# Attention and expert kernel: far and near scores set between the projections, far results stored ahead of the lower query and key rows

## The reference

```
x = layernorm(x + attention(x))     # 16 heads of 16 columns; query row n sees key rows n - d
                                    # for d in 0..32 and 48, 64, 96, 128, 192, 256, 384
x = layernorm(x + experts(x))       # router picks 2 of 8 experts for a row, 1024 places each
```

## Time and profile before

| | |
|---|---|
| median of three runs | 1755.79 us |
| profiled execution | 1759.34 us |
| its span, first to last instruction | 1757.6 us |
| PE busy | 1364.2 us (78%) |
| PE weight loads busy | 867.5 us (49%) |
| DVE, ACT, POOL busy | 971.1, 902.0, 712.1 us |
| mean granted clock of PE | 0.795 |

### The profile page before, as it was taken

One profiled execution on the slowest core, in us unless ns is written; L12 is line 12 of the kernel. 1 busy time (PEld: TensorE's weight loads), 2 busy tenths in 40 slices (PEclk: granted clock), 3 DMA queues, 4 the chain that ended last, 5 costly groups with the idle time before them and its releaser, 6 DMA issues. The chain is left out here.

```text
span 1757.6 us, 69086 instructions
## 1 busy us (share of the span) xinstructions
PE 1364.2 (78%) x31232; PEld 867.5 (49%) x31232; DVE 971.1 (55%) x2079; ACT 902.0 (51%) x1551; POOL 712.1 (41%) x653
## 2 busy tenths in 40 slices
PE   3567687787878878787887989788653999999960
PEld 1334454555545555454445555455331666666640
DVE  3225557565666656566565756657642555555426
ACT  5134454463646536465544745545543555555517
POOL 5123144363635436354443635444332133333346
PEclk9567686786968778687777868777766999999985
DMA  7655263443526344362534426253412344444239
GB/s 198 167 149 128 86 143 100 119 107 95 139 76 168 85 107 106 86 144 74 139 84 112 104 80 151 62 132 67 114 15 87 85 97 97 97 97 97 37 37 382
DMA packets 194695, 195.49 MB, mean 111 GB/s; under 512 B 61712, under 2 KB 178528, under 8 KB 191153
## 3 DMA queue, kind: packets, MB, share of 16 engines
q1 hardware_dynamic: 176208, 167.44, 36.0%
q0 software_dynamic: 15360, 15.10, 5.6%
q10 hardware_dynamic: 2832, 8.52, 1.2%
HBM read 115.63 MB, written 86.25 MB: 115 GB/s over the span
## 5 line engine op out<-in xcount | busy, mean ns | idle before, releaser
L415 POOL TENSOR_TENSOR p<-p 128x512 f16<-128x512 f32 x96 | 131.1, 1365 | 251.2 <-ACT p L833 251.1
L1172 POOL DMA_INDIRECT disp<-y,sidx x128 | 187.7, 1467 | 54.7 <-issue 38.1
L861 ACT COPY featT<-gp 128x1024 f16<-128x1024 f16 x96 | 93.2, 1027 | 219.1 <-PE gp L577 219.1
L1444 POOL DMA_INDIRECT xln<-y,place x64 | 103.4, 1615 | 223.9 <-DVE y L1584 205.4
L584 PE MATMUL gp<-featT,wr 128*128 128x512 f16 x768 | 188.9, 402 | 5.3 <-issue 2.9
L415 DVE TENSOR_TENSOR p<-p 128x512 f16<-128x512 f32 x96 | 82.5, 860 | 199.4 <-ACT p L833 199.4
L832 ACT ACTIVATE p<-st 128x512 f16<-128x512 f32 x192 | 117.3, 611 | 75.5 <-PE st L629 42.7
L1541 ACT ACTIVATE h<-up,v_near 128x512 f16<-128x512 f32 x128 | 88.2, 689 | 132.1 <-issue 124.0
L1594 DVE TENSOR_TENSOR h<-h 128x512 f16<-128x512 f32 x128 | 88.7, 694 | 74.1 <-ACT h L1542 74.1
L1159 POOL TENSOR_TENSOR x<-xin,x 128x1024 f16<-128x1024 f32 x16 | 34.0, 2127 | 235.3 <-ACT x L868 235.3
L584 PEld LDWEIGHTS gp<-featT,wr 128*128 128x128 f16 x768 | 74.1, 102 | 102.8 <-issue 27.8
(11 more groups left out here) (191 smaller groups left out, 3048.9 us busy)
## 6 DMA issues: line engine op xcount, KB each, us to landing
v_near<-v_dram SPq DMA_DIRECT2D x32, 528.0 KB, 8.1
qk_dram<-qk SPq DMA_DIRECT2D x64, 256.0 KB, 3.8
o_dram<-o_far SPq DMA_DIRECT2D x64, 136.0 KB, 4.5
o_back<-o_dram SPq DMA_DIRECT2D x16, 544.0 KB, 4.8
v_dram<-vs SPq DMA_DIRECT2D x16, 528.0 KB
v_far<-v_dram SPq DMA_DIRECT2D x64, 132.0 KB
disp<-y ACTq DMA_DIRECT2D x8, 1040.0 KB, 8.4
rows<-disp SPq DMA_DIRECT2D x16, 520.0 KB, 3.5
```

The lines of the kernel that those rows point to most:

```text
L415: engine.tensor_tensor(p16[:, b, 1, :], p32[:, b, :], p16[:, b, 0, :], ALU.subtract).then_inc(is_split, 1)
L861: gp_done(nc.scalar.copy(featT[:, i, :, :].rearrange("f c t -> f (c t)"), bank[:, :].bitcast(F16)), n, stage, PART_OF_T[stage], i)
L1172: nc.gpsimd.indirect_dma_start(out=disp[:, :], out_offset=bass.IndirectOffsetOnAxis(ap=sidx[:, t, k:k + 1], axis=0), in_=y16[n.par][:, t, ...
L1444: nc.gpsimd.indirect_dma_start(out=xln[:, :], out_offset=bass.IndirectOffsetOnAxis(ap=place[:, gr, t:t + 1], axis=0), in_=y[:, gr, t, :], ...
```

## The change

The tables move two parts of the scores on PE: the second far part (k = 1) from slot 0 to slot 1, and the first near part (k = 2) from slot 5 to slot 3. Their exponentials on ACT move from slots 1 and 5 to slots 2 and 4, and the far part's split on DVE and POOL from slot 2 to slot 3. The router's product `rank l` moves from the head of slot 3 to the end of slot 2 on PE; its place on ACT is kept by the `LATER` entry. On SP the far results are stored at slot 4 in place of 6, and the loads of the lower rows of `qs` and `ks` become a function of their own, called at slot 7.

```diff
-    0: [("proj", "qk0"), ("gate", "den1"), ("gate", "inv1")], 1: [("proj", "qk1"), ("gate", "mul")], 2: [("proj", "vg0")],
-    3: [("rank", "l"), ("proj", "vg1")], 4: [("outp", "t")], 5: [("rank", "c")],
+    0: [("proj", "qk0"), ("gate", "den1"), ("gate", "inv1")], 1: [("proj", "qk1"), ("gate", "mul")], 2: [("proj", "vg0"), ("rank", "l")],
+    3: [("proj", "vg1")], 4: [("outp", "t")], 5: [("rank", "c")],
...
-SCORES_AT = [-1, 0, 5, 8, 10, 12]
+SCORES_AT = [-1, 1, 3, 8, 10, 12]
...
             def head(n, h):
                 if (n.c, h) == (B, 2):
                     first_expert()
+                if h == 7 and n.shift(1).in_range():
+                    load_rest(n.shift(1))
                 if not n.in_range():
                     return
...
-                if h == 6:
+                if h == 4:
 
                     wait(sp, o_in, n.at(16))
                     sp.wait_ge(far_out, n.at(FAR_PAIRS, FAR_PAIRS))
...
                 for w in range(2):
                     sp.wait_ge(qk_split, n.at(4, 2 * w + 2))
                     store(n, w, 1, qk_lo_stored)
+            def load_rest(n):
+
                 sp.wait_ge(qk_lo_stored, n.at(32, 32))
                 for w, dst in ((0, qs), (1, ks)):
```

More of the change, by code:

```diff
@@ L67 @@
 AHEAD = {"split": 2, "feat": 2, "proj": 1, "maxp": 1, "gate0": 0, "gate": -1, "outp": -1, "rout": -1, "rank": -2}
-LATER = {("act", "proj", "vg0"): 2, ("act", "proj", "vg1"): 2, ("act", "gate", "mul"): 2, ("act", "rank", "l"): 3,
+LATER = {("act", "proj", "vg0"): 2, ("act", "proj", "vg1"): 2, ("act", "gate", "mul"): 2, ("act", "rank", "l"): 4,
          ("pool", "gate", "mul"): 2,
@@ L79 @@
          ("rank", "l"): 1, ("rank", "c"): 1}
-SCORES_AT = [-1, 0, 5, 8, 10, 12]
-EXP_AT = [[-1, 1, 5, 8, 11, 13], [0, 1, 5, 8, 11, 13]]
-SPLIT_AT = [1, 2, 6, 10, 12, 14]
+SCORES_AT = [-1, 1, 3, 8, 10, 12]
+EXP_AT = [[-1, 2, 4, 8, 11, 13], [0, 2, 4, 8, 11, 13]]
+SPLIT_AT = [1, 3, 6, 10, 12, 14]
 VALUES_AT = [2, 4, 7, 9, 13, 16]
```

## The result

The changed kernel takes 1797.45 us (median of 4 runs, 1786.54 to 1803.6), the kernel before 1754.8 us beside it on the same chip (4 runs). The ratio is 1.0226, with a 95% interval of 1.019 to 1.0263: slower by some 40 us. I had forecast 1769 us, +13. The direction was right, the size a third of what came.

The account below looks back on a forecast made before the run. PE was taken to bound the kernel, with its own work plus pauses for instruction blocks and waits. -45 + 22 + 27 + 14 - 15 + 10 = +13 us gave 1769 us; own range 1761 to 1784, whole range 1740 to 1801.

Parts of the forecast that it names:

- (1): Second far scores between the query and key projection halves: 29 us of pauses and 16 us of clock saved, -45 us.
- step 2: Ahead of qk0, PE waits out ACT's copies to featT, which far scores had covered: 1.5 us an iteration, +22 us.
- fourth rival: Slower: far scores keep their pauses wherever they stand, clock saved as taken; 1798 us, chance 0.08.
- third rival: Much slower: lower stacks hold up an instruction block in every iteration, one 2.78 us pause doubling; 1801 us, chance 0.12.
- (3): Ahead of the output projection, PE waits 2.3 us for featT's refill, which near scores had covered: +27 us.
- (4): Lower clock in vg1 behind narrow work and in the output projection behind the idle wait: +14 us.
- first rival: Faster: instruction blocks come in during the featT waits, so pauses behind the output projection shrink; 1731 us, chance 0.24.
- Step (5): On SP, far results stored and loaded back earlier, so PE waits less for DVE's maxima: -15 us.
- Step (6): Lower stacks' loads now run during near values and near scores, lengthening PE's pauses for instruction blocks: +10 us.

Follow-up runs that it names:

- e13: Kernel before, its second far scores done in 32 wider products instead of 128, the right scores of this part left out: 1710.47 us, ratio 0.9741.
- e16: e5 with the second far scores done in a quarter of the products, the right scores of this part left out: 1706.41 us, ratio 0.9706 to the kernel before.
- e5: Kernel before with only the second far scores moved, plus eight throwaway products ahead of the wait for featT before the first projection half: 1757.85 us, ratio 1.0011.
- e2: Kernel before with only the first near scores and rank l moved ahead of the second value and gate half: 1794.36 us, ratio 1.0225.
- e3: Kernel before with only SP's order changed, far results stored and loaded back ahead of the lower stacks: 1758.87 us, ratio 1.0002.
- e10: Kernel before with seven eighths of the lower stacks' loads left out from the third batch on: 1741.57 us, ratio 0.9945.
- e8: e2 with ACT's last value and gate copies put behind featT's refill and the output projection starting on the first copy: 1796.69 us, ratio 1.023.

## Why the prediction was right in direction and wrong in size

- **The step that failed is (1), "second far scores between the halves of the projection ... together -45 us"**, both of its terms. "I take 29 us as saved": the far scores' pauses fell by 13 us in the changed kernel (28.2 to 15.2), and pauses as a whole by under 5. I had read them rightly as blocks of instructions not yet there (the packets above), and then priced them as if they belonged to the far scores. They follow the count of instructions: moved work takes its blocks along (626.60 above), and fewer instructions made them 25 to 34 us shorter (e13 to e16). "Clock ... I take 16 us": 2.9 us came (97.7 to 94.8), and over the whole execution none (111.2 to 111.8), since the wait of step 2 lowers the clock just as the pause did; e5 shows the one, e13 the other. I named that wait as a reason to take 16 and not 22, which was far too little.
- The fourth rival, "far scores keep their pauses wherever they stand", gave 1798 us and 0.08; it is nearest to what came, though by half of its mechanism only: the pauses move on rather than stay, and the clock that it took as saved was not. The third rival gave 1801 us, near by number alone: no run shows a block held up by the lower stacks.
- **Step (2)** came out a little too small: 22 us were taken, and of 26.0 us of idle time ahead of these products in 14 iterations 23.5 are this wait and 2.5 pauses in the second half.
- **Steps (3) and (4)**, +27 and +14: e2 has both at 2.25%, or 40 us. That the sum fits is luck in part. The wait is 2.54 us where 2.3 was worked out from ACT's chain, and 35.7 us in 14 iterations for the 27 taken. The clock cost of `vg` is 15.4 us in 14 iterations, but the output projection, which step 4 had slower as well, got 5.0 us quicker. And PE's wait for the maxima, which neither step has, falls by 13 us in e2. The first rival, that waits and pauses are the same time used twice, has something in it (near values pause for 8.2 us and not 16.4), but the near maxima behind them pause more (34.1 against 25.5), and it does not decide.
- **Step (5)** was right in its place and size for SP's order alone: in e3 the maxima's wait fell by 14.2 us for 15 forecast. In the changed kernel it fell by 14.7, no more than that, though e2 has 13.1 of it without SP's order, so the two do not add up there. **Step (6)** has its +10 us without the cause that it gave: in e3 pauses behind eat step 5's gain, but neither e10 nor the packets show a block that waits for the lower stacks. The sum of both, -5, is measured as 0.

## What to carry to other kernels

Where PE waits inside runs of small matmuls at a fixed count of instructions, moving the run can just move the wait; price it by instructions and look for wider products. Before work is moved away from in front of a reader, work out from the other engine's rows when that reader's operand is ready: the cover of a copy is worth its whole length, and the clock behind it as well. When one wait is taken away by delaying an engine's work, look at what stands in order behind that work on the next engine, as POOL's addition did in e8.

## What the runs showed of the hardware

- The blocks: 3072 instructions fewer are 12 packets fewer on the instruction queue, and 46 to 54 us, some 4 us each, of which the far scores' own time is about a third in e13 (16.8 us).
- What a block costs: at the pauses of the kernel before, the next packet of instructions starts 1.0 us or more (median 1.5) after PE has gone on with the block ahead of it, takes 0.9 to 1.9 us (median 1.1), and PE goes on some 1.4 us after it has landed. Two blocks are so at least 3.46 us apart (median 4.1, where each begins with a pause). By these figures I estimate that 128 matmuls that PE gets through in under some 3.5 to 4 us end in a pause. One packet in ten starts only 4.1 to 5.5 us after PE has gone on; what holds it up is open.
- The clock can stay at 1.00 through an idle wait and fall behind it: 12 products that take 2.75 us at 618.42 took 4.33 us after the 2.69 us wait at 526.42, at a granted clock of 0.62. It need not fall at once: the 12 at 618.42 stand behind 1.67 us of waiting. Eight products with no use at all in that wait gave 14.1 us back to those behind it.
